# The five engines' order tables and the PSUM banks laid out anew in a fused mixer and FFN kernel

## The reference, cut to what matters

```python
x = x + _layernorm(attn(_layernorm(x)))          # the mixer
x = x + _layernorm(ffn(_layernorm(x)))           # the FFN

# attn: i, f, g = x@Wi.T, x@Wf.T, x@Wg.T          (512 x 512 weights)
gate = sigmoid(f);  v = silu(i) * (1.0 - gate)
o = associative_scan over t of  o[t] = gate[t] * o[t-1] + v[t]
o = o * rsqrt(mean(o*o) + EPS) * gnorm_w * g * sigmoid(g)
return o @ Wo.T
# ffn: W1, W3 are 2048 x 512, W2 is 512 x 2048
hidden = silu(x@W1.T) * (x@W3.T)
return fwht(hidden) @ W2.T                        # fwht: Walsh-Hadamard transform over 2048
```

## Time and profile before

| | us |
|---|---|
| median of 3 runs (721.26 to 724.37) | 722.8 |
| the profiled execution | 722.41 |
| its span, from the first to the last instruction | 720.6 |
| TensorE busy | 689.6 (96%) |
| DVE / ACT / POOL busy | 469.3 / 290.4 / 322.2 |
| mean granted TensorE clock, share of full | 0.983 |

### The profile page before, as it was taken

The page is one execution under the profiler, slowest core; times in us unless marked ns, Lnnn a source line. Parts: engine busy times, 40 slices in busy tenths (PEclk is TensorE's granted clock), DMA queues, the critical chain, the costliest instruction groups (busy, mean ns, idle before and its releaser), DMA issues.

```text
span 720.6 us, 11006 instructions
## 1 busy us (share of the span) xinstructions
PE 689.6 (96%) x4148; PEld 414.3 (57%) x4148; DVE 469.3 (65%) x782; ACT 290.4 (40%) x498; POOL 322.2 (45%) x268
## 2 busy tenths in 40 slices
...
GB/s 319 405 154 122 88 89 147 146 177 173 262 235 217 134 81 307 125 203 89 117 177 144 119 248 121 173 15 162 205 151 157 128 238 100 107 146 237 42 1 88
DMA packets 63717, 114.36 MB, mean 159 GB/s; under 512 B 38320, under 2 KB 42672, under 8 KB 59056
## 3 DMA queue, kind: packets, MB, share of 16 engines
...
...
## 4 chain that ended last, share of the span: by engine, by line
PE 77%; POOL 9%; DVE 5%; DMA 3%; issue 2%; SPq 2%; ACT 1%; POOLq 0%; DVEq 0%; ACTq 0%
PE ps L633 24%; PE ps L634 24%; PE ps L635 24%; PE ps L795 1%; PE ps L796 1%; DVE ring L1135 1%; SPq L563 1%; POOL ring L1440 1%; POOL ring L1438 1%; POOL ring L1436 1%; DMA ring<-W13t 1%; POOL ring L1442 1%; DMA ring<-L_attn_Wf 1%; POOL rstd L1374 1%; POOL ot L1392 1%
## 5 line engine op out<-in xcount | busy, mean ns | idle before, releaser
L633 PE MATMUL ps<-xb,ring 128*128 128x256 f16 (+1 forms) x704 | 226.9, 322 | 1.5 <-DVE ring L1135 1.2
L635 PE MATMUL ps<-xb,ring 128*128 128x256 f16 (+1 forms) x704 | 227.0, 322 | 0.0
L634 PE MATMUL ps<-xb,ring 128*128 128x256 f16 (+1 forms) x704 | 227.0, 322 | 0.0
L633 PEld LDWEIGHTS ps<-xb,ring 128*128 128x128 f16 x704 | 69.2, 98 | 49.3 <-issue 3.9
L634 PEld LDWEIGHTS ps<-xb,ring 128*128 128x128 f16 x704 | 69.0, 98 | 46.6 <-issue 2.1
L635 PEld LDWEIGHTS ps<-xb,ring 128*128 128x128 f16 x704 | 69.1, 98 | 42.8 <-issue 1.1
L1374 POOL TENSOR_TENSOR rstd<-var,neg_half 128x1 f32<-128x1 f32 x64 | 40.3, 638 | 103.8 <-DVE var L1100 38.6
L1446 POOL TENSOR_TENSOR hsp<-sga,hsp 128x512 f16<-128x512 f32 x34 | 42.0, 1238 | 98.5 <-ACT hsp L1049 98.5
L634 PE MATMUL ps<-ring 128*128 128x256 f16 x288 | 78.5, 273 | 0.0
L635 PE MATMUL ps<-ring 128*128 128x256 f16 x288 | 78.5, 273 | 0.0
L633 PE MATMUL ps<-ring 128*128 128x256 f16 x288 | 78.5, 273 | 0.0
...
## 6 DMA issues: line engine op xcount, KB each, us to landing
...
w2t<-W2t SPq DMA_DIRECT2D x8, 512.0 KB, 13.0
...
```

The lines of the kernel that those rows point to most:

```text
L633: pe.matmul(dst, a_hi, b_hi, start=start, stop=False)
L634: pe.matmul(dst, a_hi, b_lo, start=False, stop=False)
L635: return pe.matmul(dst, a_lo, b_hi, start=False, stop=stop)
```

## The change

All five tables are replaced. Every step that was in a table is in it once again: 587 steps on TensorE, 421 on ACT, 497 on DVE, 244 on POOL and 153 on SP; no step is added, dropped or given to another engine, and no function changes. So each instruction is as before in kind, size and count; only its place in its engine's queue, and the PSUM bank of a TensorE step, differ. The stated premise of the new layout is that DVE and GpSimd exclude each other operation by operation. The diff is cut to the lines of the tables that the prediction speaks of.

```diff
--- before.py
+++ after.py
 PE_ORDER = """
-XT.0.0:4 AN.0.0:5 XT.0.1:6 XT.0.2:7 XT.0.3:0 AN.1.0:1 W2N.0.0:2 AN.2.0:3 W2N.1.0 W2N.2.0 F.0.0:5 W2N.3.0 I.0.0:4
-GC.0.0:6 F.0.1:1 W2N.4.0 W2N.5.0 G.0.0:7 W2N.6.0 W2N.7.0 I.0.1:0 W2S.0.0:3 G.0.1:5 AN.3.0:6 H2.0.0:4 H2.0.1:1
-H2.1.0:7 I.0.2:2 F.0.2:3 F.0.3:6 G.0.2:0 I.0.3:5 H2.1.1:2 G.0.3:4 H2.2.0:3 H2.2.1:6 H2.3.0:0 MS.0.0:5 Y.0.0:4
-Y.0.1:1 Y.0.2:7 Y.0.3:2 ZT.0.0:5 H2.3.1:3 H2.4.0:4 WS.0.0:1 H2.4.1:6 ZT.0.1:7 ZT.0.2:2 ZT.0.3:5 H2.5.0:1
-H2.5.1:7 GA.0.0:2 UP.0.0:5 GA.0.1:0 UP.0.1:2 GA.0.2:3 UP.0.2:0 GA.0.3:5 UP.0.3:2 GA.0.4:4 H2.6.0:3 H2.6.1:0
...
-D.0.29 D.0.30 F.1.1:6 I.1.1:4 UP.0.9:7 F.1.2:6 G.1.1:4 D.0.31 I.1.2:5 I.1.3:7 G.1.2:6 D.0.32 GA.0.10:4 F.1.3:5
-G.1.3:6 D.0.33 D.0.34 UP.0.10:4 D.0.35 GA.0.11:7 MS.1.0:5 Y.1.0:6 Y.1.1:4 Y.1.2:5 Y.1.3:7 D.0.36 D.0.37
-UP.0.11:6 D.0.38 D.0.39 D.0.40 D.0.41 D.0.42 D.0.43 GA.0.12:4 UP.0.12:5 GA.0.13:6 D.0.44 D.0.45 D.0.46 D.0.47
...
-D.0.57 D.0.58 D.0.59 D.0.60 D.0.61 GP.1.0:4 GQ.1.0:5 GR.1.0:6 GP.1.1:7 GQ.1.1:4 GR.1.1:5 GU.1.0:6 GU.1.1:7
...
+XT.0.0:4 XT.0.1:5 XT.0.2:6 AN.0.0:7 AN.1.0:0 W2N.0.0:1 W2N.1.0 XT.0.3:2 AN.2.0:3 W2N.2.0 GC.0.0:4 W2N.3.0
+W2N.4.0 W2N.5.0 W2N.6.0 F.0.0:7 W2N.7.0 G.0.0:5 G.0.1:0 W2S.0.0:3 AN.3.0:4 F.0.1:6 I.0.0:2 I.0.1:7 F.0.2:1
+H2.0.0:4 H2.0.1:5 I.0.2:3 F.0.3:2 G.0.2:6 I.0.3:7 G.0.3:0 H2.1.0:1 H2.1.1:3 H2.2.0:2 H2.2.1:6 MS.0.0:7 Y.0.0:0
+Y.0.1:4 Y.0.2:5 Y.0.3:1 WS.0.0:7 H2.3.0:3 H2.3.1:0 H2.4.0:2 H2.4.1:4 ZT.0.0:5 ZT.0.1:7 ZT.0.2:1 ZT.0.3:5
+H2.5.0:7 H2.5.1:1 GA.0.0:5 UP.0.0:6 GA.0.1:5 UP.0.1:3 H2.6.0:0 H2.6.1:2 GA.0.2:5 UP.0.2:6 GA.0.3:3 UP.0.3:5
+GA.0.4:6 UP.0.4:4 H2.7.0:3 GA.0.5:5 UP.0.5:6 H2.7.1:4 GA.0.6:5 UP.0.6:7 D.0.0 D.0.1 D.0.2 D.0.3 GA.0.7:6
...
+I.1.1:6 G.1.0:7 F.1.1:4 F.1.2:5 I.1.2:7 G.1.1:4 G.1.2:5 UP.0.9:6 F.1.3:4 D.0.28 D.0.29 I.1.3:7 D.0.30 G.1.3:4
+D.0.31 GA.0.10:5 D.0.32 UP.0.10:7 D.0.33 D.0.34 MS.1.0:6 D.0.35 Y.1.0:4 GA.0.11:5 Y.1.1:6 Y.1.2:7 Y.1.3:4 D.0.36
+D.0.37 D.0.38 UP.0.11:5 D.0.39 D.0.40 D.0.41 D.0.42 GA.0.12:6 UP.0.12:7 D.0.43 GA.0.13:5 D.0.44 D.0.45 D.0.46
+UP.0.13:4 D.0.47 D.0.48 GA.0.14:6 UP.0.14:7 D.0.49 D.0.50 D.0.51 GA.0.15:5 D.0.52 D.0.53 D.0.54 D.0.55 UP.0.15:4
+D.0.56 D.0.57 D.0.58 GP.1.0:6 GP.1.1:7 D.0.59 GQ.1.0:5 GQ.1.1:4 GR.1.0:6 GU.1.0:7 GR.1.1:5 GU.1.1:4 D.0.60
+D.0.61 D.0.62 GP.1.2:6 GQ.1.2:7 GP.1.3:5 D.0.63 GR.1.2:6 GQ.1.3:4 GR.1.3:5 GU.1.2:7 GU.1.3:6 GP.1.4:7 GQ.1.4:4
...
 """
 ACT_ORDER = """
...
-G.0.3 S.0.3 H2.2.0 P.0.3 WN.5.0 WN.6.0 H2.2.1 WN.7.0 WN.8.0 WN.9.0 YN.0.0 YN.0.1 WN.10.0 WN.11.0 WN.12.0 YN.0.2
-WN.13.0 YN.0.3 ZT.0.0 WN.14.0 WN.15.0 ZT.0.1 ZT.0.2 WT.0.0 ZT.0.3 WT.0.1 H2.3.0 WT.1.0 H2.3.1 WT.1.1 WT.2.0
...
+G.0.3 S.0.3 P.0.3 H2.0.1 H2.1.0 WN.8.0 WN.9.0 WN.10.0 WN.11.0 H2.1.1 H2.2.0 WN.12.0 WN.13.0 WN.14.0 YN.0.0
+H2.2.1 YN.0.1 WN.15.0 YN.0.2 WT.0.0 YN.0.3 ZT.0.0 WT.0.1 ZT.0.1 WT.1.0 ZT.0.2 ZT.0.3 WT.1.1 H2.3.0 H2.3.1 GA.0.0
...
 """
 DVE_ORDER = """
-X1.0.0 X1.0.1 X1.0.2 X1.0.3 X2.0.0 X2.0.1 X2.0.2 X2.0.3 AN.0.0 XT.0.0 AT.0.0 XT.0.1 AN.1.0 XT.0.2 XT.0.3 AN.2.0
-AT.1.0 GC.0.0 AT.0.1 AT.2.0 GD.0.0 AT.1.1 AT.2.1 AT.2.2 GS.0.0 AT.1.2 S.0.0 W2D.0.0 AT.0.2 HN.0.0 W2S.0.0 P.0.0
-AN.3.0 AT.0.3 AT.1.3 AT.2.3 S.0.1 AT.3.0 P.0.1 H2.0.0 AT.3.1 AT.3.2 S.0.2 P.0.2 S.0.3 AT.3.3 P.0.3 H2.0.1 H2.1.0
-H2.1.1 MS.0.0 Y.0.0 H2.2.0 Y.0.1 YN.0.0 YN.0.1 Y.0.2 H2.2.1 Z1.0.0 Z1.0.1 YN.0.2 Y.0.3 Z2.0.0 YN.0.3 Z2.0.1
...
+X1.0.0 X1.0.1 X2.0.0 X1.0.2 X2.0.1 X1.0.3 X2.0.2 XT.0.0 X2.0.3 AN.0.0 GC.0.0 XT.0.1 AN.1.0 AT.0.0 AN.2.0 AT.0.1
+GD.0.0 XT.0.2 AT.0.2 XT.0.3 AT.2.0 AT.2.1 AT.2.2 W2D.0.0 AT.2.3 HN.0.0 AT.1.0 GS.0.0 AN.3.0 AT.1.1 W2S.0.0
+AT.0.3 AT.1.2 S.0.0 P.0.0 S.0.1 P.0.1 AT.3.0 AT.1.3 S.0.2 P.0.2 S.0.3 AT.3.1 P.0.3 H2.0.0 AT.3.2 AT.3.3 H2.0.1
+H2.1.0 MS.0.0 Y.0.0 H2.1.1 Y.0.1 YN.0.0 Y.0.2 H2.2.0 YN.0.1 Y.0.3 Z1.0.0 YN.0.2 YN.0.3 WS.0.0 Z1.0.1 WT.0.0
+Z1.0.2 Z2.0.0 Z1.0.3 Z2.0.1 Z2.0.2 ZT.0.0 Z2.0.3 ZT.0.1 WT.0.1 ZT.0.2 ZT.0.3 H2.2.1 WT.1.0 X1.1.0 X1.1.1 WT.1.1
+WT.2.0 H2.3.0 H2.3.1 H2.4.0 WT.2.1 UP.0.0 WT.3.0 WT.3.1 WT.4.0 UP.0.1 WT.4.1 X2.1.0 WT.5.0 WT.5.1 UP.0.2 WT.6.0
+WT.6.1 H2.4.1 UP.0.3 X1.1.2 X1.1.3 WT.7.0 WT.7.1 WT.8.0 UP.0.4 X2.1.1 XT.1.0 WT.8.1 H2.5.0 UP.0.5 H2.5.1 WT.9.0
...
 """
 POOL_ORDER = """
...
-UP.0.5 X1.1.2 UP.0.6 UP.0.7 X1.1.3 SA.1.0 SA.2.0 SA.3.0 SA.4.0 UP.0.8 P.1.0 SA.5.0 P.1.1 S.1.1 SA.6.0 P.1.2
-UP.0.9 S.1.2 S.1.3 S.2.0 P.1.3 SA.7.0 Y.1.0 Y.1.1 UP.0.10 YN.1.0 YN.1.1 Y.1.2 Z1.1.0 Y.1.3 YN.1.2 YN.1.3 UP.0.11
-Z1.1.1 Z1.1.2 Z1.1.3 ZA.1.3 ZA.1.4 ZA.1.5 ZA.1.6 UP.0.12 UP.0.13 X1.2.0 X1.2.1 X1.2.2 UP.0.14 UP.0.15 X1.2.3
...
+UP.0.4 UP.0.5 X1.1.3 UP.0.6 SA.1.0 SA.2.0 UP.0.7 SA.3.0 SA.4.0 UP.0.8 P.1.0 SA.5.0 S.1.1 P.1.1 S.1.2 P.1.2 S.1.3
+S.2.0 P.1.3 SA.6.0 Y.1.0 UP.0.9 SA.7.0 Y.1.1 YN.1.0 UP.0.10 YN.1.1 Y.1.2 Y.1.3 YN.1.2 YN.1.3 UP.0.11 Z1.1.0
+Z1.1.1 UP.0.12 Z1.1.2 Z1.1.3 ZA.1.3 ZA.1.4 ZA.1.5 ZA.1.6 UP.0.13 UP.0.14 X1.2.0 UP.0.15 X1.2.1 X1.2.2 X1.2.3
+UP.1.0 UP.1.1 V.0.0 V.0.1 V.0.2 P.2.0 V.0.3 UP.1.2 UP.1.3 S.2.1 P.2.1 UP.1.4 UP.1.5 S.2.2 P.2.2 S.2.3 UP.1.6
...
 """
 SP_ORDER = """
...
-SS.3.0 SL.6.0 SS.4.0 AS.6.0 SL.7.0 SS.5.0 SS.6.0 AS.7.0 ST.1.0 SS.7.0 LR.0.1 ST.1.1 ST.1.2 ST.1.3 ZD.1.0 ZD.1.1
-ZD.1.2 ZD.1.3 ZD.1.4 ZD.1.5 XL.2.0 XL.2.1 ZD.1.6 XL.2.2 XL.2.3 WL.1.0 WL.1.1 WL.1.2 XD.2.0 XD.2.1 XD.2.2 XD.2.3
...
+SS.2.0 SS.3.0 SS.4.0 SL.6.0 AS.7.0 SL.7.0 SS.5.0 RL.1.3 SS.6.0 ST.1.0 ST.1.1 SS.7.0 ST.1.2 WL.1.0 ST.1.3 ZD.1.0
+ZD.1.1 ZD.1.2 ZD.1.3 ZD.1.4 ZD.1.5 ZD.1.6 XL.2.0 XL.2.1 XL.2.2 XL.2.3 WL.1.1 WL.1.2 XD.2.0 XD.2.1 XD.2.2 XD.2.3
...
 """
```

More of the change, by code:

```diff
@@ new lines @@
+D.1.15 GQ.1.8:4 D.1.16 GR.1.8:6 D.1.17 GU.1.8:7 GQ.1.9:5 MS.2.0:4 Y.2.0:6 D.1.18 Y.2.1:4 Y.2.2:7 GR.1.9:5
+GU.1.9:6 D.1.19 D.1.20 Y.2.3:4 D.1.21 D.1.22 GP.1.10:5 D.1.23 GP.1.11:7 D.1.24 D.1.25 GP.1.12:5 GQ.1.10:4
+GR.1.10:6 GQ.1.11:7 D.1.26 D.1.27 GU.1.10:4 GR.1.11:7 D.1.28 D.1.29 GP.1.13:6 GU.1.11:4 GQ.1.12:5 GR.1.12:7
+GU.1.12:6 D.1.30 D.1.31 D.1.32 D.1.33 D.1.34 D.1.35 GQ.1.13:5 GP.1.14:4 D.1.36 D.1.37 D.1.38 GR.1.13:5 D.1.39
+GU.1.13:4 GP.1.15:7 D.1.40 D.1.41 D.1.42 GQ.1.14:5 GR.1.14:6 GU.1.14:4 GQ.1.15:7 D.1.43 GR.1.15:5 D.1.44 D.1.45
```

206 lines of the change are left out of this document (97 added, 109 removed).

## The result

The kernel after takes 712.9 us (median of 4 runs, 711.6 to 713.3) against 723.2 (721.3 to 724.4): ratio 0.9857, 95% interval 0.9832 to 0.9882, 10.3 us or 1.4% faster. The forecast was 717: the whole range, 709 to 724.5, holds the result, and the forecast's own range (713.5 to 719.5) misses it by 0.6. The profiled execution has a span of 711.1 us, 9.5 under the one before.

A forecast was written before the change was run, and what follows sets the result against it. TensorE, busy 689.6 of 720.6 us, was taken as the bound, with only its idle time and lowered clock to win. The sum 722.4 - 5.6 - 1.1 + 1.2 (start) + 0.5 = 717.4 gave 717, range 709 to 724.5.

The forecast's parts named there:

- S.1.3 and P.1.3 on POOL: Before MS.1.0: both go ahead of SA.6.0 and UP.0.9, so the stop at MS.1.0 and Y.1 goes; minus 5.6 us.
- UP.0.14: Hidden chunk on POOL: placed ahead of X1.2, whose statistics wait for loaded rows, so its wait goes; minus 1.1 us.
- F.0.0 later: Start: more DVE steps stand ahead of XT.0.3, which F.0.0 needs; net plus 4.5 us, bounds 2.5 and 5.5.
- rival A: Start section wins too: F.0.0 at 25.6, W2S and Y.0 stops both go; 705.4 us at best, 711 as likely; chance 0.22.
- W2S: Scale of W2 in the start: W2D on DVE no longer stands behind S.0.0, so TensorE's wait goes; minus 7 us.
- I.0.1 plus 0.5, Y.0.0 plus 1.5: Start: I.0.1 waits for AT.1.1, put far back (0.5 us); Y.0.0 for AT.3.3, behind P.0.3 on DVE (1.5 us).
- H2 between Y.0 and ZT.0: Behind Y.0.3: four H2 fill the wait, but the stop moves to small ZT steps; 0, bounds minus 4 and plus 3.
- The low clock: Start: TensorE stands before F.0.0 and around ZT; one half of a low stretch's cost taken, plus 1.7 us.
- Banks and batches 1 to 3: PSUM bank reuse and later batches: G.2.1 takes G.2.0's bank, so ACT may not be late; plus 0.5 us, bounds 0 and plus 3.
- Rival C: After GA.0.0 DVE is late for H2 and TensorE stands, if line 1260 passes a median of 1.4; 727 us, chance 0.12.
- rival D: At MS.1.0: POOL's order doesn't end the wait, since SA.5.0's raw pairs land late; 5.6 stays, 723 us; chance 0.08.
- Rival B: Start: both new stops, before F.0.0 and around ZT, bring a low clock stretch in full; 721 us, chance 0.18.

The follow-up runs named there:

- x2: Kernel after with SA.6.0 and UP.0.9 on POOL put back ahead of S.1.2, S.1.3 and P.1.3: 726.4 us, ratio 1.0068.
- x1: Kernel before with S.1.2, P.1.2, S.1.3, P.1.3 on POOL ahead of SA.6.0 and UP.0.9, and SH.6.0 on ACT behind GA.0.11: 725.5 us, ratio 1.0048.
- x5: x1 plus, on DVE, SO.6.0 behind YN.1.0 and, on ACT, SH.6.0 and SH.7.0 behind YN.1.0: 721.4 us, ratio 1.0009 to the kernel before.
- x3: Tables of after up to GA.0.0, then tables of before, SP's table all before: 718.7 us, ratio 0.9954 to the kernel before.
- y1: Kernel after with XT splits, F.0.0 and several ACT and POOL steps of the start moved earlier: 712.5 us, ratio 0.9861 to the kernel before.
- x8: Kernel after with POOL's butterflies thinned (last four of six per W2 unit on 8 columns): 713.3 us, ratio 0.9904 to the kernel before.
- x6: Kernel before with W2D.0.0 on DVE moved ahead of AT.1.2 and S.0.0: 719.9 us, ratio 0.9978.
- x7: Kernel before with POOL's butterflies thinned (last four of six per W2 unit on 8 columns): 712.5 us, ratio 0.9891.

## Why the prediction was right, and where it wasn't

In short: the terms behind GA.0.0 were right in size, two of them with half a reason. The terms of the start were too dear by some 4 us in all.

*S.1.3 and P.1.3 on POOL, minus 5.6.* The stop is gone in after and the rest as a whole won what it should, but the reason was half of it. x2 shows that the order is needed; x1 and x5 show that it wins nothing without the rest. I asked only what is next late for MS.1.0 and found S.1.3 on DVE in time. I did not ask who waits for the SA.6.0 put back: SH.6.0 on ACT, SO.6.0 on DVE, and behind it the reader of Y.1.1's bank. And SA.7.0, which was harmless in after as priced, stands in x5's way; in after Y.1.0's statistic is ahead of it. So that this term came out whole is in part luck: other moves of the change, which I hadn't credited, made it possible.

*UP.0.14, minus 1.1.* Its wait is gone, and in x3 a stop of 1.4 us stays at D.0.55. Not tried by itself.

*F.0.0 later, plus 4.5.* This step failed most. I took GC at 2.4 us and AT.0.1 and AT.0.2 at 1.72 each, from rows where POOL's butterflies run. In the new table GC stands at 16.2, ahead of the first butterfly, and took 0.8; y1 is the counter-proof: the same step 0.7 us later cost 2.6. The two splits did run beside butterflies and still took 0.78 and 0.96 in after; the same two in x8, with a thinned POOL, took 1.67 and 1.85. After, then x8:
```profile
22.42 0.78 DVE L1135 SCALAR_TENSOR_TENSOR ring<-ring,row_s 128x512 f16<-128x512 f32 x1
...
23.92 0.96 DVE L1135 SCALAR_TENSOR_TENSOR ring<-ring,row_s 128x512 f16<-128x512 f32 x1
```
```profile
21.46 1.67 DVE L1135 SCALAR_TENSOR_TENSOR ring<-ring,row_s 128x512 f16<-128x512 f32 x1
...
23.86 1.85 DVE L1135 SCALAR_TENSOR_TENSOR ring<-ring,row_s 128x512 f16<-128x512 f32 x1
```
In after it was POOL that gave way: its two butterflies from 22.73 on took 3.29 us, the first two 2.50. So a butterfly beside a split doesn't fix the split's time, and these 1.7 us are as much the luck of the moment as a fault of the price. F.0.0 came at 25.6, the time that I had given for rival A, and not at 27.5. I also counted five W2N as put ahead of F.0.0; the tables have four (W2N.3 to W2N.6), so by my own figures the term should have been plus 5.0; measured it is plus 2.9.

*W2S, minus 7.* Right that its stop goes (W2D ended at 30.4); but x6 shows that moving W2D alone is worth 1.6, and that a step that I didn't price, HN.0.0 ahead of S.0.0, belongs to it. x7 shows why S.0.0 was so long: 1.9 us without POOL's butterflies.

*I.0.1 plus 0.5, Y.0.0 plus 1.5.* I.0.1 and MS.0.0 have no wait, Y.0.0 had 0.6; from MS.0.0's start to Y.0.0's it is 0.7 more than before, against 2.0 forecast.

*H2 between Y.0 and ZT.0: 0.* From Y.0.0 to GA.0.0 it is 33.4 us, 28.8 before; H2.3.0 (1.7) came into it, so the section got 2.9 longer, at the upper bound of plus 3; in x3's profile, without the low stretch, it got 0.6 longer. WS waited 2.9 for ACT (2.5 forecast). The last ZT split on DVE ended at 98.6, not 104 to 106, since all of it began so much sooner.

*The low clock, plus 1.7.* It did not come before F.0.0, and the one at ZT was there before. x8 has it before F.0.0, so it can come there, and x3 has none at ZT with the same waits: the half chance was a fair way to price it, and which way it fell in a profile moves GA.0.0 by 2 us.

*Banks and batches 1 to 3, plus 0.5.* Nothing: no waits from 101.5 on. Rival C (H2 late on DVE) fell with line 1260's median of 0.745 against the 1.4 from which it would decide, rival D with SA.5.0, which waited but 2.5 us for its raw pair and ended at 205.6.

So the sum is off by 4.5 us (717.4 against 712.9), 3.7 of it at GA.0.0 (2.5 sooner against 1.2 later). Up to Y.0.0, H2.3.0 taken out, TensorE is 5.4 sooner (76.4 - 69.3 - 1.7), where my terms (4.5 - 7 + 0.5 + 1.5 and half of 1.7) make it 0.4 later. Of these 5.8 some 1.4 are F.0.0 (25.6 for 27.5, less the 0.5 of the miscounted W2N), 1.2 the wait ahead of F.0.1, which I gave no term and which is gone, 1.3 the waits of I.0.1 to Y.0.0, 0.9 the low clock, and 0.5 W2S, whose stop and slow matmuls were worth 7.5 rather than 7; about 0.5 I can't place. From Y.0.0 on 2.9 were given back. Rival A had the part up to Y.0.0 right, and its time, 711, was nearer than mine; but the stop behind Y.0 did not go as it had it, it moved to WS.0.0 and the ZT steps. Rival B's stop ahead of F.0.0 did not come in after.

*The rule weighed in the prediction.* GC.0.0's rows add a case: the operation with a single source in SBUF, four columns wide, also stands for a whole GpSimd operation. The Trainium skill (SBUF — State Buffer, "SBUF: two separate sides") has DVE take the shared ports with two SBUF inputs or in a two-port mode; 0.16 against 1.25 us agrees with it, if these run in such a mode, which no row here shows. That a layout would lose by taking all DVE operations as excluded was not seen: from 101.5 to 277 TensorE has no gap.
